# A two-layer AdaLN network on one core: attention with routing steps in five groups, placed between the maxima, and another order of Pool's steps and of the last batch

## The reference

```python
energy = jnp.einsum('nqhd,nkhd->nhqk', Q, K) / jnp.sqrt(jnp.float32(HEAD_DIM))
attn = jax.nn.softmax(energy, axis=-1)
out = jnp.einsum('nhqk,nkhd->nqhd', attn, V).reshape(N, S, EMBED)
...
x = x + ga * _L0_attn_ref(h, ...)
h = _layernorm(x, axis=-1) * (1 + cb) + sb
...
logits = jnp.einsum('btd,ed->bte', x, w_router)
probs = jax.nn.softmax(logits, axis=-1)
vals, idx = jax.lax.top_k(probs, TOP_K)          # 2 of 8 experts
gates = jnp.sum(jax.nn.one_hot(idx, N_EXPERTS, dtype=x.dtype) * vals[..., None], axis=-2)
y = jnp.einsum('btef,edf->bted', h, W2) + b2     # h: gelu of the first expert layer
acc = acc + jnp.einsum('bted,bte->btd', y, gates)
```

## Time and profile before

| | us |
|---|---|
| median of 3 runs | 997.61 (996.66 to 998.06) |
| profiled execution, its time | 1000.3 |
| profiled execution, its span | 998.5 |
| its mean granted TensorE clock | 0.909 |
| busy in the span: PE, DVE, ACT, POOL | 834.9, 738.9, 620.7, 503.8 |

### The profile page before, as it was taken

How to read it: one execution, slowest core, us unless ns; L and a number is a source line. 1 busy time by engine, 2 the same in 40 slices (tenths; PEclk the granted TensorE clock), 3 DMA queues, 4 the chain that set the end, 5 groups by cost and what they waited for, 6 DMA issues and landing times.

```text
span 998.5 us, 14039 instructions
## 1 busy us (share of the span) xinstructions
PE 834.9 (84%) x4566; PEld 453.7 (45%) x4566; DVE 738.9 (74%) x1530; ACT 620.7 (62%) x1095; POOL 503.8 (50%) x795
## 2 busy tenths in 40 slices
PE   5499999999988989897886999899936569878886
PEld 4232222222312222222374877677723247667774
DVE  6498888888888879782385788878749576966771
ACT  1127888888865777576484776677715836554662
POOL 4702464737255676336463067866757036753211
PEclk9659999999988999699798999999976869988997
DMA  5934736464534364202115166756360100000000
GB/s 196 189 71 159 166 120 160 132 148 145 135 120 130 101 187 116 102 23 102 61 33 182 65 236 211 250 196 207 126 243 8 25 0 1 1 1 11 22 22 32
DMA packets 45076, 110.77 MB, mean 111 GB/s; under 512 B 7806, under 2 KB 20606, under 8 KB 39494
## 3 DMA queue, kind: packets, MB, share of 16 engines
q1 hardware_dynamic: 39436, 98.33, 33.1%
q0 software_dynamic: 4992, 10.36, 3.0%
q10 hardware_dynamic: 576, 1.19, 0.4%
HBM read 57.65 MB, written 51.03 MB: 109 GB/s over the span
## 4 chain that ended last, share of the span: by engine, by line
PE 43%; DVE 18%; POOL 16%; issue 13%; ACT 6%; DMA 3%; SPq 1%; POOLq 0%; DVEq 0%; ACTq 0%
PE PS L1058 10%; POOL yd L1263 9%; PE PS L1046 7%; PE PS L1030 6%; DVE mx L882 5%; PE PS L319 2%; PE PS L1012 1%; PE PS L321 1%; PE PS L320 1%; PE PS L1068 1%; DVE cb L2301 1%; POOL X L2096 1%; POOL Gl L1255 1%; PE PS L2390 1%; PE PS L2428 1%
## 5 line engine op out<-in xcount | busy, mean ns | idle before, releaser
L882 DVE TENSOR_REDUCE mx<-PS 128x2 f32<-128x1024 f32 x256 | 305.3, 1220 | 74.6 <-PE PS L1030 67.9
L794 ACT ACTIVATE E<-PS 128x512 f32<-128x512 f32 x512 | 272.9, 597 | 83.9 <-PE PS L1046 81.0
L1046 PE MATMUL PS<-Q,K 51*128 51x512 bf16 x512 | 170.1, 404 | 12.9 <-ACT E L794 7.0
L1030 PE MATMUL PS<-K,Q 48*128 48x512 bf16 x512 | 146.2, 419 | 27.8 <-DVE mx L882 15.4
L1058 PE MATMUL PS<-E,V 128*25 128x512 f32 x1024 | 145.9, 645 | 10.2 <-ACT ov L800 9.0
L1263 POOL DMA_INDIRECT yd<-yt,goes x92 | 96.8, 1053 | 40.0 <-issue 23.7
L1046 PEld LDWEIGHTS PS<-Q,K 51*128 51x128 bf16 x512 | 37.4, 95 | 174.2 <-ACT E L794 99.0
L1427 DVE TENSOR_TENSOR Gl<-Gf,Gh 128x512 fp32r<-128x512 f32 x117 | 83.3, 728 | 26.3 <-ACT Gh L1298 14.7
L510 POOL DMA_INDIRECT xs<-HT,pos x64 | 64.8, 1012 | 74.1 <-ACT E L794 44.1
L1292 ACT ACTIVATE Gf<-PS,WR 128x512 f32<-128x512 f32 x92 | 63.1, 689 | 43.6 <-PE PS L321 32.8
L2301 DVE SCALAR_TENSOR_TENSOR cb<-ye,gt,cb 128x128 f32<-128x128 f32 x224 | 65.6, 369 | 0.0
(11 more groups left out here) (416 smaller groups left out, 1863.2 us busy)
## 6 DMA issues: line engine op xcount, KB each, us to landing
WR<-wsd SPq DMA_DIRECT2D x23, 1028.0 KB
xs<-zero SPq DMA_DIRECT2D x8, 2112.0 KB, 7.1
wsd<-wsp SPq DMA_DIRECT2D x8, 1024.0 KB, 4.1
Q<-dqk SPq DMA_DIRECT2D x16, 384.0 KB, 6.1
K<-dqk SPq DMA_DIRECT2D x16, 384.0 KB
HT<-xs SPq DMA_DIRECT2D x23, 264.0 KB
dqk<-SPL SPq DMA_DIRECT2D x31, 192.0 KB, 2.8
stage<-in_w SPq DMA_DIRECT2D x9, 516.0 KB
```

Of the source, the lines that this page charges most:

```text
L794: e.activation(E[:, m % 4, n % 4], PS[:, bank["exp", n], :], ACT.Exp).then_inc(*k.inc("exp", n))
L882: e.tensor_reduce(mx[:, 2 * s % 96:2 * s % 96 + 2], PS[:, o:o + 2, :], AX.X, ALU.max, negate=True).then_inc(*k.inc("max", s))
L1030: return e.matmul(PS[:, o + n % 2, :], Q[r, b % 3, h // 2, qt * P:(qt + 1) * P], K[r, b % 3, h // 2, :], start=True, stop=True)
L1046: e.matmul(PS[:, o, :], K[r, b % 3, h // 2, kt * P:(kt + 1) * P], Q[r, b % 3, h // 2, :], start=True, stop=True).then_inc(*k.inc("exp_mm", n))
```

## The change

- `GROUP0` has five groups: 8, 8, 8, 4 and 4 tiles. The first three are ready a batch or two earlier.
- The routing of groups 0, 1 and 2 is cut into pieces of 2 to 5 steps and one piece stands behind one maximum: places 56 to 62 of batches 2, 4, 6 and 0, 2 and 12 of 3, 5, 7, then 0 to 10 of 4 and 6 (16 to 26 of batch 7 for group 2). Group 3 is done in batch 7 at places 42 and 56, group 4 in the second stage. The ranks and ACT's two exponentials stand at place 10 of batches 3, 5 and 7.
- POOL: other places for sending (24 tiles in this stage), and in batches 6 and 7 the weights of the next expert before them.
- Batch 7: once the maxima are done, their two second banks (1 and 3) join the ring of the scores, which then has five; the two copies of `ov` go from ACT to DVE; the second half of the row maxima is written behind place 28 instead of 22.

```diff
-GROUP0 = {0: (0, 12), 1: (12, 20), 2: (20, 28), 3: (28, 32)}
+GROUP0 = {0: (0, 8), 1: (8, 16), 2: (16, 24), 3: (24, 28), 4: (28, 32)}
...
-            SENT = {5: 0, 6: 6, 7: 12}
...
                 for b in range(NB):
                     wog(b)
-                    if b >= 5:
-                        paced(b, 0, SENT[b], SENT[b] + 2)
-                        paced(b, 9, SENT[b] + 2, SENT[b] + 4)
+                    if b == 5:
+                        paced(b, 0, 0, 2)
+                        paced(b, 9, 2, 4)
+                    if b == 6:
+                        paced(b, 0, 6, 8)
+                    if b == 7:
+                        paced(b, 0, 13, 15)
+                        paced(b, 8, 15, 16)
                     max_parts(b, 1)
...
-                    if b >= 5:
-                        paced(b, 36, SENT[b] + 4, SENT[b] + 6)
-                    wsplit(b + 1)
-                    if b == 7:
-                        paced(b, 48, SENT[b] + 6, SENT[b] + 8)
+                    if b < 5 or b == 7:
+                        wsplit(b + 1)
+                    if b == 6:
+                        wsplit(b + 1)
+                        paced(b, 36, 8, 10)
+                        paced(b, 44, 10, 11)
                     if b + 1 < NB:
                         max_parts(b + 1, 0)
+                    if b == 5:
+                        wsplit(b + 1)
+                        paced(b, 58, 4, 6)
+                    if b == 6:
+                        paced(b, 56, 11, 13)
...
-                scatter(e, k, 20, 22)
+                for i, t in ((32, 16), (38, 18), (44, 20), (50, 22)):
+                    paced(NB - 1, i, t, t + 2)
...
-                        if i == 22:
+                        if i == (22 if b < NB - 1 else 28):
                             rows(b, 1)
...
-                        if i == 36:
+                        if i == 36 and b < NB - 1:
                             ovc(b, 0)
...
-                        if b in (4, 6) and i == 38:
-                            act_exp(e, k, b // 2 - 2)
-                        if b == NB - 1 and i == 46:
-                            act_exp(e, k, 2)
+                        if b in (3, 5, 7) and i == 10:
+                            act_exp(e, k, b // 2 - 1)
+                        if b == NB - 1 and i == 54:
+                            act_exp(e, k, 3)
...
+                        if b in (2, 4, 6):
+                            g = b // 2 - 1
+                            if i == 56:
+                                dve_best_value(e, k, g)
+                            if i == 58:
+                                dve_best_one(e, k, g)
+                            if i == 60:
+                                dve_second_rest(e, k, g)
+                            if i == 62:
+                                dve_second_value(e, k, g)
+                        if b in (3, 5, 7):
+                            g = b // 2 - 1
+                            if i == 0:
+                                dve_second_one(e, k, g)
+                            if i == 2:
+                                dve_chosen(e, k, g)
+                            if i == 12:
+                                dve_counts(e, k, g, bank["rk", g])
+                        if b in (4, 6) or b == NB - 1:
+                            g = 2 if b == NB - 1 else b // 2 - 2
+                            o = 16 if b == NB - 1 else 0
+                            if i == o:
+                                dve_sums(e, k, g)
+                            if i == o + 2:
+                                dve_starts(e, k, g)
+                            if i == o + 4:
+                                dve_offsets(e, k, g)
+                                dve_place(e, k, g, 0)
+                            if i == o + 6:
+                                dve_place(e, k, g, 1)
+                                dve_pos(e, k, g)
+                            if i == o + 10:
                                 dve_gates(e, k, g)
...
+                        if n + LEAD == NU:
+                            ring_a[0:0] = [(1, ("max", NU // 2 - 1)), (3, ("max", NU // 2 - 1))]
...
-                        if b in (4, 6) and i == 46:
-                            pe_ranks(e, k, b // 2 - 2, bank_d(("rk", b // 2 - 2)))
-                        if b == NB - 1 and i == 54:
-                            pe_ranks(e, k, 2, bank_d(("rk", 2)))
+                        if b in (3, 5, 7) and i == 10:
+                            pe_ranks(e, k, b // 2 - 1, bank_d(("rk", b // 2 - 1)))
+                        if b == NB - 1 and i == 54:
+                            pe_ranks(e, k, 3, bank_d(("rk", 3)))
```

More of the change, by code:

```diff
@@ L473, in dve_counts, with dve_sums @@
                           PS[:, o, 256:256 + n].rearrange("p (i e) -> p e i", e=8)).then_inc(*k.inc("rk", g))
+        def dve_sums(e, k, g):
+            tot, inc, r = counted(g)
+            over = inc.rearrange("p (e i) -> p e i", e=8)
+            n = over.shape[2]
+            k.wait_ge("const", "route")
+            k.wait_own("rk")
+            chain(k, e.tensor_tensor_scan(inc, one[:, 0:8 * n], tot, 0.0, ALU.mult, ALU.add))
+            e.tensor_copy(e8[:, 0, 1:8], over[:, 0:7, n - 1]).then_inc(*k.inc("v"))
         def dve_starts(e, k, g):
@@ L480, in dve_starts @@
             zero_, cnt, bs, base = e8[:, 0], e8[:, 1], e8[:, 4], e8[:, 5]
[L481 to L484, removed]
+            k.wait_own("v")
             e.tensor_tensor(cnt, over[:, :, n - 1], zero_, ALU.subtract)
@@ L494, in dve_places, with dve_place, dve_pos @@
             k.wait_own("v")
-            chain(k, e.tensor_tensor(w[:, 3], r.rearrange("p (i e) -> p i e", e=8), inc.rearrange("p (e i) -> p i e", e=8), ALU.add))
+            e.tensor_tensor(w[:, 3], r.rearrange("p (i e) -> p i e", e=8), inc.rearrange("p (e i) -> p i e", e=8),
+                            ALU.add).then_inc(*k.inc("v"))
+        def dve_place(e, k, g, x):
+            L, w, a, c = group(g)
+            k.wait_own("v")
+            chain(k, e.tensor_tensor(w[:, x], w[:, x], w[:, 3], ALU.mult))
+            e.tensor_reduce(posf[:, x, a:c], w[:, x], AX.X, ALU.add).then_inc(*k.inc("v"))
+        def dve_pos(e, k, g):
+            L, w, a, c = group(g)
+            k.wait_own("v")
+            e.tensor_copy(pos[:, :, a:c], posf[:, :, a:c]).then_inc(*k.inc("pos", g))
+        def dve_places(e, k, g):
+            dve_offsets(e, k, g)
             for x in range(2):
-                chain(k, e.tensor_tensor(w[:, x], w[:, x], w[:, 3], ALU.mult))
-                chain(k, e.tensor_reduce(posf[:, x, a:c], w[:, x], AX.X, ALU.add))
-            e.tensor_copy(pos[:, :, a:c], posf[:, :, a:c]).then_inc(*k.inc("pos", g))
+                dve_place(e, k, g, x)
+            dve_pos(e, k, g)
         def scatter(e, k, first, last):
@@ L1054, in pv @@
                     if m % 8 == 0 and m:
-                        k.wait_ge("ov", m // 8 - 1)
+                        k.wait_ge("ov" if b == NB - 1 and m % 16 else "ov_a", m // 8 - 1)
                     x = 9 * (g % 2)
@@ L1073, in ho @@
                 def ho(b, s):
-                    k.wait_ge("ov", 2 * b + s)
+                    k.wait_ge("ov" if b == NB - 1 else "ov_a", 2 * b + s)
                     transposes(bank_d(("otok", b, s)), ov[:, s]).then_inc(*k.inc("ho_mm", 2 * b + s))
@@ L1268, in pool @@
                 pool_hidden(e, k, NB - 1)
-                for u, first in ((0, 22), (7, 24), (11, 26), (15, 28), (18, 30)):
+                for u, first in ((0, 24), (7, 26), (15, 28), (18, 30)):
                     k.wait_ge("gelu", u)
```

123 lines of the change are left out of this document (71 added, 52 removed).

## The result

The changed kernel takes **974.75 us** (median of 4 runs, 970.19 to 976.85) where the kernel before takes 997.13 beside it: ratio 0.9765, 95% interval 0.9731 to 0.98. Measured again later on two chips, it gave 0.9766 each time (0.9721 to 0.9812; 0.9737 to 0.9796). The forecast was 978.5, the range 966 to 989. Ratios leave out runs in a slower state that the chip is sometimes in, so they can differ a little from the quotient of two medians.

What follows compares the result with a forecast made beforehand. In attention, VectorE's maxima without pause set the pace and routing steps added cost where there is no slack; 12.2 + 7.7 - 1.3 + 0.5 = 19.1 us gain, median 978.5, range 966 to 989.

Steps and rivals of the forecast that it cites:

- pieces at 56 to 2, for a group: Routing steps cut into six pieces, places 56 to 2: cost 2.4, 2.4 and 2.7 us for three groups, 7.5 in all.
- ranks in batches 3 and 5, each: TensorE's four matmuls, VectorE's two copies and a maxima buffer gone for a place: 1.0 us each, bounds 0.5 and 1.5.
- late signals, batches 5 and 6: Waits for TensorE's signals while Pool sends rows, kept since sends are moved, not removed: 2.8 us, bounds 0 and 4.
- places 0 to 10 of batch 6, less the projections that it lacks: Routing steps at the start of batch 6 cost 2.4 us; having no projections to do there gives back 2.2.
- excess, sum: Changed order's time over the undisturbed pace, batch 2 to place 8 of batch 7: 14.3 us against 26.5 before, gain 12.2.
- batch 7 from place 18: End of batch 7, where no maximum is computed: 39.23 us falls to 31.5, gain 7.7, bounds 27 and 34.5.
- of it ScalarE's wait for the max rows: Late max rows in batch 7, written behind place 28 and needed at place 32: 1.9 us lost.
- A step costs by its place: Attention routing on VectorE: a step's cost depends on where it stands, with slack at place 22 and none at 58.
- length less 0.4: The unhidden share of a routing block in a full stretch is about its length less 0.4 us.
- The rival that priced them at 1.6: Pieces hide better, 1.6 us a group, and batch 7 near its floor: time 966; below 970 got chance 0.12.
- the floor: Batch 7 from place 18: ScalarE's busy 25.7 us less the 0.6 copy of ov, 25.1.
- The rival of the clock: TensorE's clock falls in batches 2 to 6 from more short interruptions, making the kernel slower, 1009 us at 60; chance 0.05.

Runs made afterwards that it cites:

- the second control: The changed kernel again, unedited, on a third chip beside a word-for-word repeat of the kernel with three score banks: 975.41 us, ratio 0.9766.
- the block run: Changed kernel with the steps of best, second and chosen in one block behind place 56 of batches 2, 4 and 6: 982.26 us, ratio 0.9835.
- the moved one: Kernel before, with Pool splitting the last expert's weights ahead of its four sends at place 36 of batch 7: 986.83 us, ratio 0.9892.
- the four variants: Changed kernel with, separately, SyncE's order changed, four sends moved, batch 7's row maxima earlier, three score banks: 1001.43, 999.3, 999.56 and 997.52 us.

## Why the prediction held, step by step

The medians differ by 22.4 us; the forecast was 19.1. The profiled spans differ by 30.1, since the profiled execution of before (1000.3) was longer than its other runs and that of after was the shortest of its runs. 25.9 of the 30.1 are in batches 2 to 7 and 1.0 in the tail; 1.9 before batch 2 and 1.3 behind attention have nothing to do with the change. Against the profile of the second control batches 2 to 7 differ by 22.0. Sizes below are from the first profile, batches 2 to place 8 of batch 7 first.

| term | forecast | measured |
|---|---|---|
| pieces at 56 to 2, for a group | 2.4 to 2.7 | 1.28 (first two groups) |
| places 0 to 10 of batch 4 | 1.8 | 0.86, and 1.3 more where the clock falls |
| ranks in batches 3 and 5, each | 1.0 | 1.43 |
| late signals, batches 5 and 6 | 2.8 | 0 (not 0 on one chip) |
| places 0 to 10 of batch 6, less the projections that it lacks | 0.2 | -1.6, what is left of the sum |
| stall at the end of batch 5 | not foreseen | 3.43 |
| excess, sum | 14.3 | 9.4 |
| ranks, places 8 to 18 of batch 7 | 1.3 lost | 1.62 lost |
| batch 7 from place 18 | 7.7 won | 10.4 won |
| of it ScalarE's wait for the max rows | 1.9 | 2.43 |
| tail | 0.5 | 1.0 |

- **"A step costs by its place"** is right, and the block run shows it: the same steps cost 1.28 in pieces and about 4.4 in one block. By the "length less 0.4" a block costs 3.2; the rest is about what the clock takes that falls behind it. (The steps are sixteen, not eighteen, but they take 3.57 us in the block, so the 3.6 stands.) What I mis-sized is the pieces' cover. I took a full stretch as one in which only the places around 0 and 2 hide something; the pieces hid 2.3 of 3.6 us. The rival that priced them at 1.6 was nearest.
- **The missed term** is SyncE's queue. I wrote that the send at place 36 of batch 5 goes, and did not follow what stands behind Pool's new last step there: `store_w` waits for the split, and the max rows wait behind `store_w`. Before, the split ended at 367.9 and the rows were written only at 370.6, so the same order cost little. Of the 3.43 us some 0.7 goes with the sends (batch 5 at 53.69 without them).
- **Batch 7**: the size came out 2.7 better, and the shares were partly misread. The stall for the max rows and the clock behind it were foreseen at 1.9 and 1.5, and taking that stall away is worth 3.3 (28.21 to 24.88). Inside the 1.9, the 0.8 for the rows to land was too low: they were issued by 437.54, and the exponential at 439.46 follows its score by 0.4, so 1.5 passed. Too high were the waits for features and logits and the late signals, 3.0 together: with the stall gone all that is left over the floor is 0.5. In the account of before, the banks, the routing wait and the low clock stood as parts that add. The runs show one cause for most: the split on the routing is worth 7.9 of 38.6 (30.69 in the moved one). The banks, with the copies on VectorE, then take 30.69 to 24.88.
- **Pool** had its margin: it ended 2.3 us before VectorE where I said some 5, and is over by 1.2 at the floor where I said "about 1".
- **The sends** were the largest error of reading. I kept 2.8 and 1.5 us for them on both sides as something moved and not removed. Not quite half of the gain is that the changed kernel doesn't suffer from its sends as the one before did: outside batch 4, 12.0 of 25.9 by the first profile, 9.4 of 22.0 by the control's. The larger part of that is the split of batch 7, which the sends only pushed.
- **The rival of the clock** I gave 0.05, and as a whole it didn't come. But its mechanism is there, and "low clock only behind long stalls" was too narrow: at place 10 of batches 4 and 6 the clock falls after nothing longer than the short waits of places 2 to 10, in five of the nine other profiles of this order in one batch or both, and costs 1.3 each time. By the Trainium skill ("TensorE: Matmul & The Clock Gate", A second HAM failure mode: psum-queue depth-cycling) frequent short idles between groups of matmuls make the clock swing; these traces agree for two places, not for batches 2, 3 and (up to its stall) 5, which have 1.00. No run shows what decides it.
- **Luck**: that 19.1 came so near 22.4 is partly luck. The stall of 3.4 that was not foreseen is hidden by pieces and late signals that were priced too high, and 966 to 989 was wide enough for both.

## What to carry to other kernels

Ask what a step waits behind, and what it will run beside, as well as how long it runs: two large effects here, 8 us in batch 7 of before and 3.4 in batch 5 of after, came from the place of one Pool step, and showed in VectorE's steps and in SyncE's queue. Cut work for a full engine into pieces (here under 1 us each) and spread them over places; the same steps in a block cost over three times as much here, the clock that fell behind the block included. When variants of a kernel all come out slow at once, run one of them word for word again beside the control before believing any of them.

## What was not expected of the hardware

- The same program took 0.9967 of the kernel before on one chip and 0.9843 on another. On the first the four variants had waits for a remote signal of up to 9.1 us on ScalarE while Pool sent rows, in batch 7, and in the clearest case VectorE and ScalarE went on together. The kernel before itself differed by only 2.5 us between these chips. No run shows where the signals are held up, and whether the changed kernel without sends would be free of them on that chip wasn't tried.
- A low clock multiplies a small stall. In batch 7 of the kernel before, two steps that took 3.85 us instead of 0.45 were followed by 17 us at 0.50, and with them at 0.45 batch 7 was 8.0 us shorter.
